# Fold of the product-key query weights with the keys split over two norms, and three DVE settings of the self-attention moved

## What is computed

```python
# self-attention, layer 0 (16 heads of 16; random features beside local softmax)
qkv = (x @ Wqkv_w.T + Wqkv_b).reshape(b, l, 3, H, DH)
...
out = einsum(local_score, v) + global_out * g_prime_scale
return ctx @ out_w.T + out_b
# feed-forward, layer 0 (product keys: 8 heads, 2 x 64 keys of 128, best 8 of 64 x 64 experts)
xn = _rmsnorm(x, norm_w)
q = (xn @ w_q.T).reshape(b, t, H, 2, DK)
sim1 = jnp.einsum('bthd,hkd->bthk', q[..., 0, :], keys[:, :, 0, :])
sim2 = jnp.einsum('bthd,hkd->bthk', q[..., 1, :], keys[:, :, 1, :])
...
hidden = gelu(einsum(xn, expert_down[fi])) * relu(fs)
return einsum(hidden, expert_up[fi])
# the whole
x = x + xattn0(layernorm(x), ctx);  x = x + attn0(layernorm(x));  x = x + ffn0(layernorm(x))
x = x + xattn1(layernorm(x), ctx);  x = x + attn1(layernorm(x));  x = x + ffn1(layernorm(x))
```

## Time and profile before

| what | us |
|---|---|
| median of 3 runs | 459.45 |
| lowest, highest run | 456.75, 459.59 |
| the profiled execution's own time | 459.85 |
| span of its profile | 458.0 |
| TensorE busy (matmul) | 429.9, 94% |
| TensorE weight loads busy | 308.5, 67% |
| VectorE busy | 276.7, 60% |
| ScalarE busy | 172.3, 38% |

### The profile page before, as it was taken

One profiled execution on the slowest core, in us unless ns is written; L12 is line 12 of the kernel. 1 busy time (PEld: TensorE's weight loads), 2 busy tenths in 40 slices (PEclk: granted clock), 3 DMA queues, 4 the chain that ended last, 5 costly groups with the idle time before them and its releaser, 6 DMA issues.

```text
span 458.0 us, 8353 instructions
## 1 busy us (share of the span) xinstructions
PE 429.9 (94%) x3124; PEld 308.5 (67%) x3124; DVE 276.7 (60%) x945; ACT 172.3 (38%) x443; POOL 6.3 (1%) x9
## 2 busy tenths in 40 slices
PE   2999999999999899977899999999899999899997
PEld 2645555555555488955658889888745669787774
DVE  7256676766767645687779989610325556465333
ACT  2346656646666502778322330000123233324110
POOL 5000000000000000000000000000000000000000
PEclk9999999999999899999999999999999999999999
DMA  8500000100005906200049800009493000000000
GB/s 297 156 2 1 1 0 2 34 2 1 1 1 186 370 4 243 124 1 3 1 137 375 286 1 5 1 3 308 102 358 111 1 0 3 0 1 0 1 1 23
DMA packets 21704, 36.09 MB, mean 79 GB/s; under 512 B 1694, under 2 KB 18464, under 8 KB 21024
## 3 DMA queue, kind: packets, MB, share of 16 engines
q1 hardware_dynamic: 21664, 35.55, 22.6%
HBM read 35.29 MB, written 0.26 MB: 78 GB/s over the span
## 4 chain that ended last, share of the span: by engine, by line
PE 49%; issue 42%; DVE 5%; ACT 2%; POOL 1%; POOLq 0%; DVEq 0%
PE bank L858 6%; PE bank L823 6%; PE bank L849 6%; PE bank L1056 6%; PE bank L945 5%; PE bank L920 3%; PE bank L925 2%; PE bank L1070 2%; PE bank L813 2%; PE bank L934 1%; PE bank L1074 1%; PE bank L709 1%; POOL region_d L1889 1%; DVE region_g L1522 1%; PE bank L724 1%
## 5 line engine op out<-in xcount | busy, mean ns | idle before, releaser
L1128 ACT ACTIVATE region_g<-bank,nm_new 128x512 f32<-128x512 f32 (+1 forms) x64 | 40.0, 630 | 35.9 <-DVE nm_new L1398 34.8
L1393 DVE CUSTOM_DVE_ANT_0 bank<-bank,bias_h 128x512 f32<-128x512 f32 (+1 forms) x64 | 38.7, 646 | 7.3 <-issue 7.3
L555 PEld LDWEIGHTS bank<-ident,region_g 128*128 128x128 f32 x230 | 24.5, 140 | 21.9 <-issue 12.8
L589 PE MATMUL bank<-region_a,qT 64*128 64x512 f32 (+1 forms) x128 | 32.5, 568 | 0.8 <-ACT region_g L1128 0.8
L555 PE MATMUL bank<-ident,region_g 128*128 128x128 f32 x230 | 32.5, 281 | 0.6 <-ACT region_d L1114 0.6
L348 ACT ACTIVATE root<-var 128x2 f32<-128x2 f32 x6 | 1.2, 204 | 80.4 <-DVE var L358 80.4
L572 PE MATMUL bank<-region_d,region_a 128*64 128x256 f32 x248 | 31.1, 390 | 0.0
L858 PE MATMUL bank<-region_u,region_g 128*128 128x256 f32 x128 | 28.7, 382 | 0.0
L1114 ACT COPY region_d<-bank 128x384 f32<-128x384 f32 (+1 forms) x50 | 24.8, 531 | 9.8 <-PE bank L555 9.8
L823 PE MATMUL bank<-xnT,region_d 128*128 128x256 f32 x128 | 28.0, 379 | 0.0
L823 PEld LDWEIGHTS bank<-xnT,region_d 128*128 128x128 f32 x128 | 24.2, 190 | 3.7 <-issue 0.5
(11 more groups left out here) (341 smaller groups left out, 796.1 us busy)
## 6 DMA issues: line engine op xcount, KB each, us to landing
region_d<-in_downT SPq DMA_DIRECT2D x2, 2048.0 KB, 9.7
region_u<-in_up SPq DMA_DIRECT2D x2, 2048.0 KB, 11.4
region_a<-in_ctx SPq DMA_DIRECT2D x1, 3072.0 KB, 13.5
region_d<-in_w_q SPq DMA_DIRECT2D x1, 2048.0 KB, 11.7
region_d<-in_ctxT SPq DMA_DIRECT2D x1, 2048.0 KB, 8.7
region_d<-in_ctxT SPq DMA_DIRECT2D x2, 1024.0 KB, 15.1
region_u<-in_wg SPq DMA_DIRECT2D x1, 1728.0 KB, 7.0
region_u<-in_wu SPq DMA_DIRECT2D x1, 1728.0 KB, 10.7
```

What stands on the lines that cost most here:

```text
L555: mm = nc.tensor.transpose(bank[4 + e][:, k * P:(k + 1) * P], prob[:, u % 2, e, k * P:(k + 1) * P], ident[:, :])
L589: mm = nc.tensor.matmul(bank[2 * s + e][:, 0:size], lhsT=qT[own, p, t * P:(t + 1) * P], rhs=keys[own, p, 0:size], start=True, stop=True)
L1128: nc.scalar.activation(prob[:, u % 2, e, 0:tiles * P], bank[2 * s + e][:, 0:tiles * P], ACT.Exp, scale=-1.0, bias=nm_new[:, p, t, e:e + 1] ...
L1393: ins = nc.vector.tensor_tensor_reduce(bank[2 * s + e][:, 0:size], bank[2 * s + e][:, 0:size], bias_h[:, t, 0:size], -1.0, 3e38, ALU.add, ...
```

## The change

- `w_q3` becomes two tiles of 16 x 128 columns: the first half of each row of `w_q` in `region_d` at 0, the second in `region_u` at 5248 (where `alpha` of the cross-attention was). Each is loaded by a transfer of its own (1 MB instead of 2): the first where the whole stood, the second after `y_psum` 1, counted by a new semaphore `sim2_in`.
- TensorE does half c = 0 of the fold (32 matmuls, banks 3 and 2) at the first place, then 4 spare transposes, then turns x. It does half c = 1 (32 matmuls, banks 6 and 7) at the second place, where the 26 spare transposes stood.
- ScalarE copies two banks at the first place, one before `keep_first` at the second place, one after its half of the turned x. TensorE waits for these copies ahead of the similarities of each half of the columns (`wsim_ready` 3, then 4).
- SyncE: the down weights wait for `wsim_psum` 2 instead of 4; `iota` and the up weights wait for `wsim_psum` 4 beside `x_ready` 3.
- VectorE: the memset in `region_a` and the halving of the biases stand before the wait for `y_psum` 1 instead of after the norm; the two memsets in `v2` stand after the squared queries.

```diff
--- before.py
+++ after.py
@@ -160,7 +160,8 @@
         att_flat = part(region_g, 4160, TT * D).rearrange("p (t n) -> p t n", t=TT)
         attT = sb("attT", [P, DC, T])
 
-        w_q3 = part(region_d, 0, 4096).rearrange("p (g d) -> p g d", g=2 * EH)
+        w_q3 = [part(region, at, 2 * EH * P).rearrange("p (g d) -> p g d", g=2 * EH)
+                for region, at in ((region_d, 0), (region_u, 5248))]
         keysT = part(region_u, 4224, 1024)
         downT = region_d[:, :].rearrange("p (c e) -> p c e", c=DC)
         up = region_u[:, :].rearrange("p (h d) -> p h d", h=ET)
@@ -320,6 +321,7 @@
             sem(n) for n in ("sim_psum", "down_psum", "gelu_ready", "chosen_ready", "chosenT_psum"))
         hit_ready, hot_ready, mixw_psum, hidden_ready = (
             sem(n) for n in ("hit_ready", "hot_ready", "mixw_psum", "hidden_ready"))
+        sim2_in = sem("sim2_in")
         lin_in, norm_done = sem("lin_in"), sem("norm_done")
         qk2_psum, q2_ready, k2_ready, v2_psum, v2_ready = (
             sem(n) for n in ("qk2_psum", "q2_ready", "k2_ready", "v2_psum", "v2_ready"))
@@ -464,12 +466,15 @@
             for dst, name in ((proj, "proj"), (minus_half, "minus_half"), (mixT, "mixT"), (qk_bias[:, :], "qk_bias")):
                 sp.dma_start(dst, a[name]).then_inc(lin_in, 16)
             sp.dma_start(band, a["band"].rearrange("p (t k) -> p t k", t=TT)).then_inc(lin_in, 16)
-            sp.dma_start(w_q3, a["w_q"].rearrange("(g p) d -> p g d", p=P)).then_inc(sim_in, 16)
+            sp.dma_start(w_q3[0], a["w_q"].rearrange("(g p) d -> p g d", p=P)[:, :, 0:P]).then_inc(sim_in, 16)
             sp.dma_start(keysT, a["keysT"]).then_inc(sim_in, 16)
-            sp.wait_ge(wsim_psum, 4)
+            sp.wait_ge(y_psum, 1)
+            sp.dma_start(w_q3[1], a["w_q"].rearrange("(g p) d -> p g d", p=P)[:, :, P:D]).then_inc(sim2_in, 16)
+            sp.wait_ge(wsim_psum, 2)
             for c in range(DC):
                 sp.dma_start(downT[:, c], a["downT"][c * P:(c + 1) * P]).then_inc(experts_in, 16)
             sp.wait_ge(x_ready, 3)
+            sp.wait_ge(wsim_psum, 4)
             sp.dma_start(iota, a["iota"]).then_inc(iota_in, 16)
             for c in range(2):
                 sp.dma_start(up[:, c * 16:(c + 1) * 16], a["up"].rearrange("(h l) d -> l h d", l=P)[:, c * 16:(c + 1) * 16]
@@ -640,19 +645,21 @@
             mm.then_inc(y_psum, 1)
 
 
-            pe.wait_ge(sim_in, 32)
-            for c in range(DC):
+            def key_weights(c):
+
                 for g in range(2 * EH):
                     mm = nc.tensor.matmul(bank[(3, 2, 6, 7)[2 * c + g // EH]][:, (g % EH) * NK:(g % EH + 1) * NK],
-                                          lhsT=w_q3[:, g, c * P:(c + 1) * P], rhs=keysT[:, g * NK:(g + 1) * NK],
+                                          lhsT=w_q3[c][:, g, :], rhs=keysT[:, g * NK:(g + 1) * NK],
                                           start=True, stop=True)
                     if g % EH == EH - 1:
                         mm.then_inc(wsim_psum, 1)
 
-            turn_xn(pe, 2, (bank[0], bank[1]))
+            pe.wait_ge(sim_in, 32)
+            key_weights(0)
+            turn_xn(pe, 2, (bank[0], bank[1]), spare=4)
             pe.wait_ge(lin_in, 128)
             pe.wait_ge(xnT_ready, 4)
-            pe.wait_ge(wsim_ready, 4)
+            pe.wait_ge(wsim_ready, 2)
             for m in range(8):
                 for c in range(DC):
                     mm = nc.tensor.matmul(bank[2 + m // 2][:, (m % 2) * T:(m % 2 + 1) * T],
@@ -804,11 +811,16 @@
             turn_and_project(pe, 1, att_flat, (0, 1), wo2, (2, 3))
 
 
-            turn_xn(pe, 3, (bank[0], bank[1]), spare=26)
+            pe.wait_ge(sim2_in, 16)
+            key_weights(1)
+            turn_xn(pe, 3, (bank[0], bank[1]))
             pe.wait_ge(xnT_ready, 6)
             pe.wait_ge(x_ready, 3)
+            pe.wait_ge(wsim_ready, 3)
             for t in range(TT):
                 for half in range(2):
+                    if half == 1:
+                        pe.wait_ge(wsim_ready, 4)
                     for c in range(DC):
                         mm = nc.tensor.matmul(bank[2 + 2 * t + half][:, :], lhsT=xnT[:, c, t * P:(t + 1) * P],
                                               rhs=w_sim[:, c, half * 512:(half + 1) * 512],
@@ -1158,10 +1170,13 @@
                 turned_half(-1, 1, e, TILES[1], n_turns * 64)
 
             take_root(act, 2)
-            for k in range(4):
+            def copy_key_weights(k):
                 act.wait_ge(wsim_psum, k + 1)
                 nc.scalar.copy(w_sim[:, k // 2, (k % 2) * 512:(k % 2 + 1) * 512], bank[(3, 2, 6, 7)[k]][:, :]
                                ).then_inc(wsim_ready, 1)
+
+            copy_key_weights(0)
+            copy_key_weights(1)
             act.wait_ge(xnT_psum, 3)
             nc.scalar.copy(xnT[:, 0, :], bank[0][:, 0:T]).then_inc(xnT_ready, 1)
             for m in range(4):
@@ -1232,10 +1247,12 @@
 
 
             take_root(act, 3)
+            copy_key_weights(2)
             keep_first(act, 3, (2, 3))
             act.wait_ge(xnT_psum, 5)
             nc.scalar.activation(xnT[:, 0, :], bank[0][:, 0:T], ACT.Copy, scale=column("L0_ffn_norm_w", 0)
                                  ).then_inc(xnT_ready, 1)
+            copy_key_weights(3)
             for b in range(ET // 2):
                 act.wait_ge(down_psum, b + 1)
                 nc.scalar.activation(hidden[:, 2 * b:2 * b + 2, :],
@@ -1465,6 +1482,9 @@
             scale_output(XP - 1)
             dve.wait_ge(rows_in, 16)
             add_bias("L0_xattn_bo")
+            nc.vector.memset(part(region_a, 4096, 2048), 0.0)
+            dve.wait_ge(lin_in, 128)
+            step(nc.vector.tensor_scalar(qk_bias[:, 0:8], qk_bias[:, 0:8], 0.5, None, ALU.mult))
             dve.wait_ge(y_psum, 1)
             dve.wait_ge(bias_added, 1)
             for t in range(TT):
@@ -1474,11 +1494,6 @@
 
 
             layer_norm(dve, step, kept, xn, after=xn_ready)
-            nc.vector.memset(v2[:, :, :, 16:17], 1.0)
-            nc.vector.memset(v2[:, :, :, 17:32], 0.0)
-            nc.vector.memset(part(region_a, 4096, 2048), 0.0)
-            dve.wait_ge(lin_in, 128)
-            step(nc.vector.tensor_scalar(qk_bias[:, 0:8], qk_bias[:, 0:8], 0.5, None, ALU.mult))
             dve.wait_ge(xnT_psum, 4)
             nc.vector.tensor_copy(xnT[:, 1, :], bank[1][:, 0:T]).then_inc(xnT_ready, 1)
             for m in range(4):
@@ -1487,6 +1502,8 @@
                                         qk_bias[:, m:m + 1], ALU.mult, ALU.add).then_inc(q2_ready, 1)
             dve.wait_ge(q2_ready, 4)
             nc.vector.tensor_tensor(q2sq, q2T, q2T, ALU.mult).then_inc(q2_ready, 1)
+            nc.vector.memset(v2[:, :, :, 16:17], 1.0)
+            nc.vector.memset(v2[:, :, :, 17:32], 0.0)
             dve.wait_ge(v2_psum, 1)
             nc.vector.tensor_tensor(v2[:, :, :, 0:16], bank[0][:, :].rearrange("p (t h d) -> p t h d", t=TT, h=LH),
                                     row("L0_attn_v_b").rearrange("p t (h d) -> p t h d", h=LH), ALU.add
```

## The result

The changed kernel takes 456.68 us (median of 20 executions, 453.22 to 457.80), the kernel before 459.53 (20 executions, 456.75 to 462.48). The ratio is 0.9922, 95% interval 0.9904 to 0.9939: 3.6 us or 0.8% faster, which lies inside 1%. The two medians differ by 2.9 us and the two means by 3.4; the spread of the executions, which is the subject of experiments 5 to 8, makes the difference between these figures. A ratio leaves out executions more than 1.5% above the fastest of their kernel (one, of the split alone). The forecast was 456.4 us, from -3.1. The profiled execution of the changed kernel took 456.38 with a span of 454.6, 3.4 us less than the span before.

What follows compares the result with a forecast made beforehand. TensorE, with matmuls busy 94% of the span, was taken to bound the kernel. First place -3.2 and second place +0.1 gave -3.1 us, from 459.45 to 456.35, rounded 456.4; range 453.7 to 459.4 us.

Steps and rivals of the forecast that it cites:

- First place, -3.2: Fold ahead of the turn of x: half the fold lets queries and keys start 3.2 us earlier, bounds 2.9 to 3.3.
- VectorE's settings: Memset and bias halving fit the 5.16 us idle ahead of L1471, `v2` settings the 3.04 us idle; cost nothing.
- the gain without the move: First place with VectorE's settings left behind the norm: VectorE free only at 174.76, so only 1.0 us won.
- Second place, +0.1: 32 fold matmuls instead of 26 transposes ahead of the similarities: cost 0.1 us, bounds 0 to 0.6.
- the lower bound: Second place costs 0: the 0.1 us delay may vanish where the choice's turn holds TensorE 0.22 us at L832.
- The rival of the table load: Second place pays more: table load ahead of ScalarE's last copy, or added waits, 0.85 plus some 0.1; 457.3 us; chance 0.09.
- Transfers: Halves of `w_q` and the down weights land before they are wanted, 50 us of cover for the later ones; cost nothing.
- The gain carries: Rival: a wait behind the first place not tied to it swallows 2 to 3 us, say 459; chance 0.06.
- The clock: Rival: shorter dense block with the gap near 172.6 brings falls to 1.2 GHz, 461.4 us; chance 0.04.
- More than forecast: Rival: more runs in the kernel's faster mode, perhaps without the dip at 157 (up to 1.6 us); 453.7; chance 0.15.

Runs made afterwards that it cites:

- experiments 5 to 8: Spare transposes in TensorE's idle stretches of the changed kernel (455.33; 454.60; 455.84; 454.53 us), in 6 also of the kernel before (458.06) and the split without the move (458.95).
- the split alone: Changed kernel with VectorE's three settings back behind the norm, so only the fold is split; 460.63 us, ratio 1.0009 to the kernel before.
- the longer block: Changed kernel with 20 spare transposes instead of 4 behind the half fold at the first place; 457.72 us, ratio 0.9973 to the kernel before.
- `no_second_fold`: Changed kernel with 26 spare transposes instead of the fold's second half at the second place, similarities reading the first half twice; 456.53 us, ratio 0.9913.
- `split_filled`: The split alone plus spare transposes in TensorE's idle stretches near 157, 200 and 413 us; 458.95 us, ratio 0.9987; run again 459.55, ratio 0.9967.
- `split_gap_filled`: `split_filled` plus 18 spare transposes behind the turn of x at the first place, inside the 2.74 us idle; 457.38 us, ratio 0.9937.
- the settings alone: Kernel before with only VectorE's settings moved, the fold whole at the first place; 459.63 us, ratio 1.000.

## Why the prediction was right

The mechanism was right at both places, and four runs bear it out: the split without the move, the move without the split, the longer block, and the second place without its fold. That the median came within 0.3 us of the forecast is in part luck, as it hangs on how many falls of the clock the executions had.

- *First place, -3.2.* Measured -3.20, and each term: the fold's 32 loads in 3.62 us (forecast 3.60), the start 1.07 us after the normed x (forecast 1.11: 1.01 and 0.1 for the spare transposes).
- *VectorE's settings.* The memsets were said to be covered at both new places; 3.05 and 2.50 us of idle remain there. That the gain without the move would be only 1.0 was measured as 1.03 at the place.
- *Second place, +0.1.* Measured +0.12 at the place, and the lower bound, that the turn of the choice takes it back, came true for 0.10 of it. `no_second_fold` shows the same 0.13. The rival of the table load is out: it comes behind the copy.
- *Transfers.* The two halves of `w_q` landed 9.7 and 5.4 us after their issue; the first was wanted at 167 and the second not before 226. No engine waited for them.
- *The gain carries.* From the queries and keys to the second block 53.70 us both times.
- *The clock.* This rival did not come true for this kernel: the changed kernel leaves 0.56 us of idle at the first place and its profile shows no fall there. An idle of 2.74 us there does bring falls in most executions, as `split_filled` (17 of 20) and `split_gap_filled` (0 of 9) show. The same split without the move and without filling had more falls than the kernel before, which turned a gain of 1 us into none; its own profile has them at other places, so for that kernel the link is not shown. I had costed "the split without the move" at -1.0 in time; that step was wrong by the falls, 2.1 us in the median.
- *More than forecast.* The faster level of 453.7 was real (5 of 20 executions, 453.6): they are the executions without any fall, at 157 us or elsewhere. I had priced that fall at up to 1.6 us; at its place it costs 1.58. The distance from the executions with one fall (456.4) is 2.8, and the profiles suggest where most of the other 1.2 us lie. At the beginning of the span the first queries run in part at half the rate, and for how long differs from one execution to the next. The lines are the changed kernel's and the longer block's, whose code is the same up to there:

```profile
11.75 7.90 PE L526 MATMUL bank<-xnT,region_a 128*128 128x256 f32 x32
```

```profile
11.38 7.17 PE L526 MATMUL bank<-xnT,region_a 128*128 128x256 f32 x32
```

In the first the second, third and fourth of these matmuls start 0.43 us apart and the late ones 0.22, in the second all from the second on 0.22. They end at 19.65 and at 18.55, 1.1 us apart. The windows show no lower clock here. In the three unfilled profiles with the fall at 157 they end at 19.24 to 20.07, in the three without it at 18.54 to 18.76. Two of the three filled profiles without any fall have a long beginning too (19.24 and 19.43), so it does not need a fall to go with it. No execution of the changed kernel at 0.999 was profiled, so this is argued and not shown.

The measured ratio says 3.6 us, the places 3.1. By level of the clock the difference, to all 82 executions of the kernel before that ran beside the experiments, is 3.1 without a fall (456.7 and 453.6), 3.0 with one (459.4 and 456.4) and 3.2 with two (460.2 and 457.0). These agree with the places. The rest of the 3.6 is the mix of levels, and the interval (2.8 to 4.4 us) holds both.

## What to carry to other kernels

Where a norm or another short chain stands between two TensorE stages, look how long TensorE's own work in front of it is: work that doesn't depend on the chain is free up to the chain's length and is paid beyond it, so divide it among several such places. Shorten a block only together with whatever else ends at the same time (here VectorE's settings); otherwise the gain becomes an idle stretch, and an idle stretch of TensorE can cost more on top of itself through the clock (here 1.7 us for a fall behind 2.74 us of idle). And compare executions of the same granted clock: a difference of 3 us at a spread of 6 is plain within a level. A level counts the falls and does not place them; for that a profile is needed.

## What was not expected of the hardware

A single idle of 2.74 us in front of full work was followed by 3 us at 1.2 GHz in the second profile of `split_filled`, and by none in its first or in that of the split alone; several short idles (TensorE busy for 2.24 of 4 us) did the same. The fall began in the work behind the idle and cost 1.6 to 1.7 us. Of 20 executions of `split_filled` three had no fall, and of 9 with the idle filled all had none.

The beginning of the kernel differs from execution to execution as well: the first queries took 7.17 to 7.90 us, with matmuls 0.43 us apart ahead of those 0.22 apart. The Trainium skill, "TensorE: Matmul & The Clock Gate" (Part 1), says that activity releases the slow clock and that the number of slow matmuls at a kernel's start varies from run to run; these traces agree.

Why a given execution falls at 157 and another at 200 and 413 stays open. The same idle stretch does not always bring a fall: 1.44 us of idle ahead of the score matmuls near 198 us was followed by one in the profile of the settings alone and by none in the changed kernel's.
